# Graph network kernel on one Trainium2 core: who announces gathered rows, SyncE or GpSimd

## The reference, cut

```python
h = relu(layernorm(x))
# layer 0: attention over 8 heads of 64
e = leaky_relu(el[src] + er[dst]); a = softmax of e over the edges of each dst
x = x + segment_sum(feat_v[src] * a, dst)
# layer 1: two graph convolutions, W1 and W2
h = relu(layernorm(x))
for W, b in ((W1, b1), (W2, b2)):
    t = h @ W
    h = relu(segment_sum(t[src] * dinv[src] * dinv[dst], dst) + 2 * dinv**2 * t + b)
x = x + h
```

## Time and profile before

| what | us |
|---|---|
| median of 3 runs | 5374.18 |
| lowest, highest | 5372.75, 5381.17 |
| profiled execution, its own time | 5383.65 |
| its span, first to last instruction | 5381.5 |

### The profile page before, as it was taken

The page is one execution under the profiler, slowest core; times in us unless marked ns, Lnnn a source line. Parts: engine busy times, 40 slices in busy tenths (PEclk is TensorE's granted clock), DMA queues, the critical chain, the costliest instruction groups (busy, mean ns, idle before and its releaser), DMA issues.

```text
span 5381.5 us, 82588 instructions
## 1 busy us (share of the span) xinstructions
PE 3719.0 (69%) x15674; PEld 2068.6 (38%) x15675; DVE 2792.5 (52%) x4907; ACT 2086.3 (39%) x5120; POOL 2651.4 (49%) x2782
## 2 busy tenths in 40 slices
PE   4430399866676777779767676777797766777764
PEld 3210398345555555654322222222343222222221
DVE  6300298855665666677444444444553444444445
ACT  3100165134444444445334343434443343444444
POOL 2667300055555555543365565656403666565653
PEclk8765699988988888989888888889898888888987
DMA  7610022365555555555555555555514555555557
GB/s 241 139 46 5 20 60 77 128 185 160 167 160 155 156 153 148 160 147 184 171 172 164 162 172 165 168 156 168 149 68 156 168 170 166 162 166 164 172 163 240
DMA packets 327907, 798.07 MB, mean 148 GB/s; under 512 B 85656, under 2 KB 107818, under 8 KB 326921
## 3 DMA queue, kind: packets, MB, share of 16 engines
q0 software_dynamic: 201376, 631.37, 40.7%
q1 hardware_dynamic: 109241, 134.08, 7.8%
q10 hardware_dynamic: 17232, 31.99, 2.0%
HBM read 712.03 MB, written 84.78 MB: 148 GB/s over the span
## 4 chain that ended last, share of the span: by engine, by line
PE 46%; issue 25%; DVE 8%; another core or an unknown queue 7%; DVEq 4%; SPq 4%; ACT 3%; DMA 2%; ACTq 0%; POOL 0%; POOLq 0%
PE mm L1648 13%; PE tr L1648 10%; PE mm L1477 5%; DVE big L862 3%; PE mm L1626 3%; PE mm L1570 3%; PE sm L1626 3%; SPq L1079 3%; PE tr L1570 3%; PE sm L1514 2%; DVE edge L836 2%; PE tr L1626 1%; PE hist_ps L1626 1%; ACT eler_hots L1397 1%
## 5 line engine op out<-in xcount | busy, mean ns | idle before, releaser
L1274 POOL DMA_INDIRECT edge<-h_tab,row_idx x1564 | 1481.9, 948 | 1223.0 <-SPq L1085 543.9
L1648 PE MATMUL mm<-edge,eler_hots 128*128 x1664 | 945.1, 691 | 571.0 <-issue 320.9
L1397 ACT ACTIVATE eler_hots<-eler_hots,ones 128x256 f32<-128x256 f32 x1272 | 639.2, 502 | 1389.4 <-PE mm L1648 521.8
L1648 PE MATMUL tr<-edge,eler_hots 128*128 x1664 | 900.0, 666 | 172.5 <-issue 102.1
L1274 POOL DMA_INDIRECT rows_wmat<-v_tab,row_idx x782 | 740.8, 947 | 558.6 <-SPq L1085 347.5
L862 DVE TENSOR_TENSOR big<-big,mm 128x512 f32 x832 | 571.8, 687 | 724.3 <-PE mm L1648 439.0
L1388 ACT ACTIVATE eler_hots<-iota,ndrel 128x128 f32<-128x128 f32 x2544 | 882.0, 393 | 157.5 <-issue 0.7
L862 DVE TENSOR_TENSOR big<-big,tr 128x512 f32 x832 | 571.8, 687 | 643.7 <-PE tr L1648 255.4
L1648 PEld LDWEIGHTS mm<-edge,eler_hots 128*128 128x128 f32 x1664 | 326.3, 212 | 1140.8 <-issue 1139.9
L1648 PEld LDWEIGHTS tr<-edge,eler_hots 128*128 128x128 f32 x1664 | 347.6, 215 | 690.4 <-issue 689.1
L1626 PE MATMUL mm<-edge,eler_hots 128*128 128x260 f32 x1176 | 419.0, 442 | 257.5 <-ACT eler_hots L1397 154.5
(11 more groups left out here) (242 smaller groups left out, 3531.7 us busy)
## 6 DMA issues: line engine op xcount, KB each, us to landing
h_tab<-rows_wmat SPq DMA_DIRECT2D x98, 256.0 KB, 2.0
edge<-h_tab,row_idx POOLq DMA_INDIRECT x1564
rows_wmat<-low_tab SPq DMA_DIRECT2D x133, 128.0 KB
ht_tab<-rows_wmat SPq DMA_DIRECT2D x49, 256.0 KB
big<-ht_tab ACTq DMA_DIRECT2D x49, 256.0 KB
v_tab<-rows_wmat ACTq DMA_DIRECT2D x49, 256.0 KB
x_tab<-big SPq DMA_DIRECT2D x49, 256.0 KB, 3.0
rows_wmat<-v_tab,row_idx POOLq DMA_INDIRECT x782
```

The lines of the kernel that those rows point to most:

```text
L1274: pool.indirect_dma_start(ring[:, 2 * u + i, :], None, tab, bass.IndirectOffsetOnAxis(ap=row_idx[:, b, n:n + 1], axis=0)).then_inc(a["rows ...
L1397: act.activation(onehot[:, s.j % 2, :, :], dist[:, :, :], ACT.Relu, bias=ones[:, 0:1], scale=-1.0).then_inc(a["onehot_set"], 1)
L1648: pe.matmul(sum_ps[bank][:, :], onehot[:, s.j // 2 % 2, s.j % 2, :], edge[:, ds(slot[0][s.j], D)], start=True, stop=True).then_inc(a["step ...
```

## The change

`relay` no longer waits for rows and no longer adds to `rows_ready`. `gather` on POOL does: before it issues unit g it waits until unit g-3 has landed (`TELL` is 3) and adds one to `rows_ready`. After the last unit it does so for the last three. SP still loads row numbers, and for that waits for `rows_ready` to reach g+1; it still passes on freed slots. With the lag of 3 the straight part ahead of POOL's loop is 48 steps long instead of 24.

```diff
+TELL = 3
@@ relay, on SP
                 def step(s):
-                    g, u = s.k, s.j % units
-                    sp.wait_ge(a["rows_in"][u], s.turn * (2 * PER_IDX // units * 32) + (s.j // units * 32 + 32 + a["rows_before"][u]))
-                    sp.sem_inc(a["rows_ready"], 1)
+                    g = s.k
                     if s.j % PER_IDX == 0 and (s.inner or g + PER_IDX < UNITS):
+                        sp.wait_ge(a["rows_ready"], g + 1)
                         load_idx((s.turn * 2 + (s.j // PER_IDX + 1)) * IDX, (s.j // PER_IDX + 1) % 2)
...
                 pipelined(sp, UNITS, 2 * PER_IDX, 0, step)
+                sp.wait_ge(a["rows_ready"], UNITS)
@@ gather, on POOL
+                def tell(s):
+                    u, back = (s.j - TELL) % a["units"], (TELL - s.j - 1) // a["units"] + 1 if s.j < TELL else 0
+                    landed = s.turn * (2 * PER_IDX // a["units"] * 32) + (
+                        ((s.j - TELL) // a["units"] if s.j >= TELL else -back) * 32 + 32 + a["rows_before"][u])
+                    pool.wait_ge(a["rows_in"][u], landed)
+                    pool.sem_inc(a["rows_ready"], 1)
+
                 def step(s):
+                    if s.past(TELL):
+                        tell(s)
+                    if not s.live():
+                        return
                     g, u, b = s.k, s.j % a["units"], s.j // PER_IDX
                     if s.past(a["units"]):
                         wait_alone("pool", pool, a["slot_free"], g - a["units"] + 1)
...
-                pipelined(pool, UNITS, 2 * PER_IDX, 0, step)
+                pipelined(pool, UNITS, 2 * PER_IDX, TELL, step)
```

## The result

| | kernel before, us | changed kernel, us |
|---|---|---|
| median, 4 runs each | 5377.68 | 5455.34 |
| lowest, highest | 5372.75, 5401.94 | 5403.56, 5470.67 |
| profiled execution's span | 5381.5 | 5465.8 |

The ratio is 1.0119, with an interval of 1.0082 to 1.0155: the change made the kernel 1.2% slower. The ratio goes by all runs, 64 us by their means; the medians lie 78 us apart. The prediction said 5336 us.

A forecast was written before the change was run, and what follows sets the result against it. No engine fills a stage; consumers and POOL wait for each other through the ring, SyncE's order making `rows_ready` late. -39 + 0 + 0 + 1 = -38 us; from the median 5374.18, 5336 us; range 5260 to 5388.

The forecast's parts named there:

- (2): In the three aggregations, a quarter of the consumers' removed waits on `rows_ready` comes through as time: -39 us.
- The 158 us: DVE's and PE's waits on `rows_ready` exposed to the change: 83.5 + 97.4 - 22.8, in 65 waits.
- the whole is wrong if slow stretches grow: Sign in the aggregation windows: slow stretches grow in number or length, busy shares fall, no new wait to name.
- (1): At `rows_ready`, announcing is uncoupled from consumers' progress and SyncE's loads; nearly all 158 us of waits go.
- (3): POOL's added wait, increment and register arithmetic per unit run under the gather before: 0 us.
- (4): POOL's wait for landing of unit g-3 is just met, with 0.28 us to spare, and costs nothing.
- (5): At a stage's start and end, first announcement not later, units 1 and 2 perhaps 1 us later: +1 us in all.
- (6): SyncE's index load now waits for POOL's announcement of unit g, for indices needed twelve units later: nothing.
- Rival C: In GAT, the ring is too short for announcing three late after SyncE's load bursts: +22, 5396 us; chance 0.12.
- D: At POOL's landing wait, landings slower than 6.3 us under load stall each unit: well above 5400 us; chance 0.04.
- A: Consumers' waits vanish but return as other waits or longer slow stretches: 5374 us, within 11 us; chance 0.24.

The follow-up runs named there:

- e12: Changed kernel with a POOL memset after each unit's two gathers, awaited before the next two; 5902.75 us, ratio 1.0916 to the kernel before, on a slow chip.
- r2_after: Changed kernel run again unaltered, on a slow chip; 5480.1 us against 5412.18 for the kernel before, ratio 1.0135.
- e7: Kernel before with each of SyncE's bursts of register loads done three times; 4325.72 us, ratio 1.0439 to the kernel before.
- e8: Changed kernel with each of SyncE's bursts of register loads done three times; 4159.76 us, ratio 1.0036 to the kernel before.
- r1_after: Changed kernel run again unaltered, on a quick chip; 4145.4 us against 4141.19 for the kernel before, ratio 1.0008.
- g1: Kernel before with a small POOL memset after each 4 gathers, on a slow chip; 5446.3 us, ratio 1.0124 to the kernel before.
- g2: Changed kernel with a small POOL memset after each 4 gathers, on a slow chip; 5467.61 us, ratio 1.0171 to the kernel before.
- e1: Kernel before with POOL also waiting for the landing of unit g-3, SyncE still announcing; 4149.38 us against 4147.43, ratio 1.0006, on a quick chip.
- e11: Changed kernel with TELL at 4 instead of 3; 4138.79 us against 4139.27 for the kernel before, ratio 0.9997.
- g4: Changed kernel with a POOL memset after each 4 gathers, also ahead of the first stage, on a slow chip; 5474.44 us, ratio 1.0173 to the kernel before.

## Why the prediction was wrong

**The step that failed is (2)**, "what that is worth", -39 us. It measured +87 us in the stages. That the named waits vanish was right. That a quarter of them comes through took the slow stretches as given, a speed at which each engine works for itself. They are not: they depend on how POOL spaces its gathers (e12 in its stages against r2_after). That a consumer which no longer waits for announcements changes when slots come free, and so when POOL issues, is argued and not shown. The 158 us themselves were read from a trace that lacks a third of the increments; counted from the instructions, less the first units, they are about 130. The prediction wrote the outcome down as "the whole is wrong if slow stretches grow", with no chance and no price, and set its bounds for the step at 0 and -158 us, with none above zero. A sign could not come out of it.

(1) Uncoupling: right. DVE's real waits went from 71.3 us to 0.1, PE's from 83.1 to 28.1, the first units among them. e7 and e8 show the mechanism where SyncE alone is slow, 166 us.

(3) POOL's instructions cost nothing: right (r1_after, 1.0008 with POOL as the bound; the median gap between gathers is 0.30 us in every trace of the two kernels).

(4) The wait for landing costs nothing: right at three late on both kinds of chip, at four on the quick ones. My row of a first gather, 5.98 us, is 2.3 us longer than one in the steady state, 3.6 to 3.7. The figure of the Trainium skill (DMA: Bandwidth & Descriptors, "Anatomy of one DMA"), by which I estimated 2.6 us, fits better: counted from the end of the second gather, 0.95 us after its start, the landing takes 2.7. I had weighed it against the wrong row.

(5) Right for the first unit: in the first GCN stage it lands, and is announced at once, 7.3 us after the first gather's start both before and after. (6) SyncE waits 2.7 us once for POOL before an index load; its price of nothing stands.

Rival C is false at three late, on slow chips too (DVE's 0.1 us), and true at five on quick ones (+73 us in GAT). D is false: POOL hardly stalls on landings. A named the way in half a sentence, "longer slow stretches, since POOL, served sooner, gathers on without a pause", but priced it at zero.

**What stays open.** Why does the change add standstill? I had this theory: slots come free in bunches, POOL's series are longer, so the others stand longer. For it: gathers in series of ten or more with gaps under 0.6 us rose from 133, 267 and 244 a stage to 229, 394 and 378, and standstill depends on POOL's spacing. Against it: on quick chips 770 to 782 gathers of a stage lie in such series, and nobody stands; and in r2_after the first stage has 166 in such series, little more than before's 133, yet is 41 us longer. With the spacing of g1 and g2 the change still costs 21 us, 0.4%, instead of 68 to 78; the two intervals overlap, though each run of g2 is above each of g1. The gap is smaller because the kernel before became slower (+63 us), not because the changed one became faster. So it is shown that the loss occurs only on slow chips, inside the stages, where all engines but POOL start less, and that such standing vanishes with enough room between POOL's gathers. It is not shown which detail of the change brings more of it: neither POOL's wait alone (e1) nor another lateness than three was run on a slow chip. Nor is it known what makes a chip slow, or whether the recording takes part. No version beat both kernels: e11 equals the kernel before on a quick chip (0.9997), and on slow chips the kernel before is the fastest of all that ran.

## What to carry to other kernels

A wait that the profile names can be removed with a sure mechanism (here 166 us where it stood alone) and the time still not come back, if the waiting engine's pace is set by something without a name. When a profile shows stretches in which several engines slow down at one moment, first find what the one busy engine does there, and give any change that touches that engine's rhythm a price on both sides of zero. And let an experiment's own timeline show that the pause or wait that it adds is the size that was meant, before its result is read.

## What the runs showed of the hardware

- The same kernel takes 4139 to 4147 us in some groups of runs and 5378 to 5412 in others. The difference shows as standing and crawling of PE, DVE, ACT and SP beside POOL's back-to-back indirect DMAs: a stage takes 978 us or 1232 to 1298, and the part ahead of the first stage about 705 us (e1_wait_only) or 1094 (the kernel before).
- The slow traces lack a third to a half of the increments of `rows_ready` (788 recorded of 1173 before, 564 after), the quick ones next to none; e12's stages, slow but with pauses, hold 1169.
- On the slow chips a slow stretch begins some 5.7 us (median, before and in r2_after; there the middle half is 4.4 to 7.1) after POOL resumes gathering behind a gap of over 1 us, and where POOL stops it ends some 1.6 us (median) after its last gather.
- A high load of the DMA engines is not needed for it: ahead of the first stage, with short gathers, their share was 0.11, with 18 GB/s, and PE was busy 57 of 330 us (window 290 to 620 us of the kernel before); in r1_after, quick and by then further on in its program, PE was busy 312 us of the same window.
- A distance of 1.46 us after each two gathers, 0.97 of it with POOL idle, removes it (e12); 0.65 us after each four does not (g1, g2, g4).
- Where all instructions of an engine's queue take 0.7 us, the releaser that the profile names for its next matmul can be merely the last event seen: 10.49 us before 3043.85 were put down to an increment, and the wait for it took 51 ns.
- A landing: 3.6 to 3.7 us from the gather's start in the steady state (r1_after, the middle half of its gathers), 5.98 for the second gather of the first GCN stage (the kernel before).
